# Short rows scattered to first-choice places inside the fused stage; the first pass scatters sums only; both passes run as one stream of 80 pairs

## The chip, the cores and the metric

The kernel runs on one core of one Trainium2 chip. The metric is device time in microseconds (us), the median of three runs. PE is the matrix engine, ACT, DVE and POOL are the scalar, vector and GpSimd engines, and SP is the engine that issues most DMAs (transfers) here. A scatter is an indirect DMA issued by POOL: 128 rows, one per partition, each written to the row of a DRAM tensor that an index in SBUF names.

## The reference

8192 tokens (32 batches of 256) of width 256 go through one layer. Only its second half is touched by the change:

```python
x = x + tanh(g_xattn) * attention(layernorm(x), ctx)      # first stages
y = layernorm(x)                                          # (8192, 256)
scores = softmax(y @ Wg.T); wk, idx = top_k(scores, 2)    # 16 experts, 2 chosen
h = einsum('td,edh->teh', y, W1); h = u * silu(g)         # HID = 128
z = sum over the 2 chosen experts of wk * (h_e @ W2[e])
ys = gated(y @ Ws1) @ Ws2                                 # shared expert
out = x + tanh(g_ffn) * (z + ys)
```

## The kernel before

The program has four stages with a barrier of all engines between them: `prepare` (weights), `attend` (attention, writes x1 to DRAM), `mix` (the fused stage: shared expert, router, placing) and `passes` (routed experts).

**mix** runs 16 steps G of 512 tokens (four tiles of 128). A row in SBUF has ROW = 2 * D + 4 = 516 numbers: the running sum x + shared expert (columns 0 to 255), the normalised y (256 to 511) and a tail of four (token number, first-choice place, and the two weights). The rows lie in NX = 5 buffers `row[G % 5]`. DVE makes the tail: `place(G)` (L1336) computes both places, `weigh(G)` (L1324) the two weights; `add_x1(G)` (L1363) adds the shared expert's output one step later, and its semaphore is `added`. POOL writes the token number (`note`, L1100), makes the low halves of expert G's weights (`low_weights`, L1104, 128x768) and scatters the four tiles of step G-1 to their second-choice places in `rows1` (`scatter`, L1109, the DMA on L1116). SP loads the rows of step G+3 into their buffer once the scatters of step G-2 from that buffer have landed; ACT normalises them (`normalise`, L1243). The order on each engine is written out by hand.

**passes** runs over pairs: a pair q is two tiles of 128 places that each belong to one expert. Pass 1 has pairs 0 to 39 (second choices, from `rows1`), pass 2 pairs 40 to 79 (first choices, from `rows0`). Rows lie in U = 10 buffers `prow`. A step s of the pipeline does, in this order, the transposes of pair s (L1549), the hidden matmuls of pair s-1, the transposes of pair s-2 and the down matmuls of pair s-3 on PE; ACT and DVE split each result in high and low halves; DVE's last operation of a pair (L1666, two instructions, semaphore `final`) adds weight times result to the sum in the row. POOL then scatters: in pass 1 the whole row of 516 to its first-choice place in `rows0`, in pass 2 the sum (256) to `out`. SP loads pair q into buffer q % 10 when pair q-10's scatters have landed. Unused places are covered by blank tiles (`blank_tails`, L1441): 16 for `rows1` at the end of mix, 16 for `rows0` in four groups within pass 1. Between the passes SP waits for every scatter of pass 1, since any tile of `rows0` may hold rows from any of them; PE runs 18 idle matmuls (L349) there. PE's expert addresses are register loads once in ten pairs.

## Time and profile before

| | us |
|---|---|
| median of 3 runs | 992.02 (991.86 to 994.16) |
| the profiled execution | 994.32 |
| its span, first to last instruction | 992.5 |
| mix, from its first POOL instruction to POOL's last scatter | 495.9 to 712.3 |
| pass 1, first transpose to last | 718.6 to 842.2 |
| pass 2, first transpose to last | 862.5 to 970.7 |
| PE busy in the span | 919.1 (93%) |
| POOL busy in the span | 495.0 (50%) |

A profile tells for one execution when each instruction ran on each engine, and what ended an engine's idle time. A busy share over the span mixes stages, so the stages are read apart. "us from issue to landing" is the time from the issue of a DMA to its semaphore. The granted clock (PEclk) is PE's clock as a share of 2.4 GHz. The span leaves out some 2 us around the program that the run's time has.

### The profile page before, as it was taken

To read this page: it belongs to the slowest core of one execution; us is meant where nothing else is said; L and a number is where in the kernel's file an instruction comes from. 1 tells how busy PE (TensorE), PEld (TensorE's weight loads), DVE (VectorE), ACT (ScalarE), POOL (GpSimd) and SP (SyncE) were. 2 spreads that over 40 slices of the span, in tenths; PEclk is the share of its full clock that TensorE was granted. 3 is DMA by queue.
4 is the path that set the end of the run, shared out by engine and by line. 5 is a ranking of instruction groups with operands and counts; after the bars stand their busy time and mean duration, and the time that the engine had idled before them with its cause. 6 is when DMAs were issued, how large, how long until landed. Compare 5 with 4: busy or idle time off the path is not lost. (4 is left out here: it accounts for less than half of the span.)

```text
span 992.5 us, 20889 instructions
## 1 busy us (share of the span) xinstructions
PE 919.1 (93%) x6722; PEld 854.1 (86%) x6722; DVE 806.0 (81%) x1840; ACT 524.2 (53%) x1191; POOL 495.0 (50%) x604
## 2 busy tenths in 40 slices
PE   6699999999999999999779999998797889899994
PEld 6599999999999999998768888887597889699993
DVE  7899999999999999988568989988476568278773
ACT  6577776777777775644254455553043334144441
POOL 4346354453645355343434555554346457457765
PEclk9799999999999999999779999999999889999997
DMA  8213323332233222221153444443799998478880
GB/s 238 73 47 105 91 61 92 92 105 66 86 92 105 71 68 72 70 71 44 38 192 107 171 168 164 169 161 121 273 317 350 336 353 279 148 256 269 264 279 27
DMA packets 108342, 151.15 MB, mean 152 GB/s; under 512 B 21830, under 2 KB 72394, under 8 KB 108240
## 3 DMA queue, kind: packets, MB, share of 16 engines
q1 hardware_dynamic: 92880, 107.60, 35.0%
q0 software_dynamic: 15360, 42.24, 11.2%
q8 instruction: 59, 0.97, 0.4%
q14 instruction: 43, 0.35, 0.1%
HBM read 90.19 MB, written 65.90 MB: 157 GB/s over the span
## 5 line engine op out<-in xcount | busy, mean ns | idle before, releaser
L671 POOL TENSOR_TENSOR prob<-prob,row_sum 128x616 f32<-128x616 f32 x64 | 77.9, 1217 | 141.9 <-DVE row_sum L893 141.9
L1527 POOL DMA_INDIRECT rows_scratch<-prow x80 | 78.7, 984 | 66.2 <-DVE prow L1666 37.2
L1116 POOL DMA_INDIRECT rows_scratch<-row,slot x64 | 67.9, 1061 | 75.4 <-DVE row L1367 60.7
L1527 POOL DMA_INDIRECT out<-prow x80 | 78.7, 984 | 49.7 <-issue 26.8
L1624 ACT ACTIVATE eyT_hi<-ps_ey 128x512 fp32r<-128x512 f32 x80 | 47.9, 599 | 105.2 <-PE ps_ey L1549 105.2
L75 PE MATMUL ps_h<-w_flat,eyT_hi 128*128 x320 | 97.5, 305 | 0.0
L1649 DVE TENSOR_TENSOR eyT_lo<-ps_ey,eyT_hi 128x512 fp32r<-128x512 f32 x80 | 55.3, 692 | 49.0 <-ACT eyT_hi L1624 46.2
L76 PE MATMUL ps_h<-w_flat,eyT_hi 128*128 x320 | 90.6, 283 | 0.0
L77 PE MATMUL ps_h<-w_flat,eyT_lo 128*128 x320 | 90.5, 283 | 0.0
L75 PE MATMUL ps_s<-M_hi,xT_hi 128*128 128x308 f32 x256 | 82.0, 320 | 7.4 <-PEq L387 4.1
L805 ACT ACTIVATE prob<-prob,rstd 128x616 f32<-128x616 f32 x64 | 51.9, 811 | 67.4 <-DVE prob L883 67.4
L261 POOL TENSOR_TENSOR xT_lo<-xT_raw,xT_hi 128x512 fp32r<-128x512 f32 x32 | 41.2, 1287 | 88.2 <-ACT ctxb_hi L227 87.1
L232 DVE TENSOR_TENSOR PT_lo<-ps_pt,PT_hi 77x512 fp32r<-77x512 f32 x128 | 80.2, 666 | 0.0
L75 PE MATMUL ps_o<-PT_hi,V_hi 96*128 96x256 f32 x256 | 76.7, 300 | 3.4 <-DVE PT_lo L232 3.3
L76 PE MATMUL ps_s<-M_lo,xT_hi 128*128 128x308 f32 x256 | 79.0, 308 | 0.0
L77 PE MATMUL ps_s<-M_hi,xT_lo 128*128 128x308 f32 x256 | 78.7, 308 | 0.0
L75 PE MATMUL ps_o<-wo_hi,OT_hi 128*128 128x256 f32 x256 | 75.8, 296 | 1.4 <-DVE OT_lo L232 1.4
L76 PE MATMUL ps_o<-PT_lo,V_hi 96*128 96x256 f32 x256 | 73.4, 287 | 0.0
L77 PE MATMUL ps_o<-PT_hi,V_lo 96*128 96x256 f32 x256 | 73.4, 287 | 0.0
L76 PE MATMUL ps_o<-wo_lo,OT_hi 128*128 128x256 f32 x256 | 73.0, 285 | 0.0
L77 PE MATMUL ps_o<-wo_hi,OT_lo 128*128 128x256 f32 x256 | 72.5, 283 | 0.0
L1666 DVE SCALAR_TENSOR_TENSOR prow<-ps_z,prow 128x256 f32<-128x256 f32 x160 | 69.4, 476 | 1.2 <-PE ps_z L77 1.1
(283 smaller groups left out, 3338.8 us busy)
## 6 DMA issues: line engine op xcount, KB each, us to landing
prow<-rows_scratch SPq DMA_DIRECT2D x160, 258.0 KB, 3.6
rows_scratch<-blank SPq DMA_DIRECT2D x34, 258.0 KB, 3.8
xT_raw<-in_xT SPq DMA_DIRECT2D x32, 256.0 KB, 4.5
x_tok<-in_x SPq DMA_DIRECT2D x32, 256.0 KB, 2.8
x_scratch<-x_tok SPq DMA_DIRECT2D x32, 256.0 KB, 3.1
row<-x_scratch SPq DMA_DIRECT2D x16, 512.0 KB, 3.9
x_ahead<-in_x SPq DMA_DIRECT2D x26, 256.0 KB, 4.4
w_raw<-in_W SPq DMA_DIRECT2D x16, 256.0 KB, 3.5
```

The lines of the kernel that those rows point to most:

```text
L75: nc.tensor.matmul(out, lh, rh, start=start and n == 0, stop=False)
L76: nc.tensor.matmul(out, lh, rl, start=False, stop=False)
L77: last = nc.tensor.matmul(out, ll, rh, start=False, stop=stop and n == len(pairs) - 1)
L232: nc.vector.tensor_tensor(lo, source, f32(hi), ALU.subtract).then_inc(done, 1)
L261: nc.gpsimd.tensor_tensor(a.xT[par][1][:, :, :], a.xT_raw[par][:, :, :], f32(a.xT[par][0][:, :, :]), ALU.subtract).then_inc(a.x_split, 1)
L671: nc.gpsimd.tensor_tensor(pr, pr, row_sum[i][:, :].unsqueeze(2).broadcast_to((P, H, CK)), ALU.mult).then_inc(normed, 1)
L805: nc.scalar.activation(prob[i][:, :], prob[i][:, :], ACT.Exp, scale=c.rstd1[:, bass.ds(2 * b + i, 1)]).then_inc(exp_done, 1)
L1116: pool.indirect_dma_start(c.rows1, bass.IndirectOffsetOnAxis(slot1[:, t:t + 1], 0), row[G % NX][:, i, :], None).then_inc(scattered[G % NX] ...
L1527: pool.indirect_dma_start(dram, bass.IndirectOffsetOnAxis(target, 0), row[u][:, i, 0:columns], None, bounds_check=bound, oob_is_err=False) ...
L1624: nc.scalar.activation(yT[p][0][:, :, :], ps_y[p][:, :, :], ACT.Copy).then_inc(yT_hi, 1)
L1649: V.tensor_tensor(yT[p][1][:, :, :], ps_y[p][:, :, :], f32(yT[p][0][:, :, :]), ALU.subtract).then_inc(yT_lo, 1)
L1666: last = V.scalar_tensor_tensor(row[b][:, i, 0:D], ps_z[p][:, i, :], row[b][:, i, weight:weight + 1], row[b][:, i, 0:D], ALU.mult, ALU.add)
```

## The change

Every token's short row (y and tail, 260 numbers) is scattered to its first-choice place in `rows0` already in mix, by four more scatters per step. Pass 1 then scatters only the sum (256 numbers) to the same place of a new tensor `sums0`. Pass 2 loads both parts apart: short rows need only the buffer, `rows0`'s blanks, and nothing of pass 1; the sums need all of pass 1's scatters, and only DVE's last operation waits for them (`sum_in`). The loops become one stream of 80 pairs, without the idle matmuls between. The blanks in pass 1 cover both tensors, so they are twice as many of half the size. In the last step of mix some DVE and ACT operations change places, and several semaphores are shared that were apart. POOL's loops are written out.

```diff
 (mix, SP and POOL)
-                    wait(sp, scattered[u], 64 * (G // NX))
+                    wait(sp, scattered[u], 128 * (G // NX))
...
+                def scatter_short(G):
+                    pool.wait_ge(noted, G + 1)
+                    pool.wait_ge(weighed, G + 1)
+                    for i in range(4):
+                        pool.indirect_dma_start(
+                            c.rows0, bass.IndirectOffsetOnAxis(tail_of(G)[:, i, 1:2].bitcast(I32), 0),
+                            row[G % NX][:, i, D:], None).then_inc(scattered[G % NX], 16)
+
                 for G in range(STEPS + 1):
                     if G < STEPS:
                         note(G)
                         low_weights(G)
+                    if G == STEPS - 1:
+                        scatter_short(G)
                     if G >= 1:
                         scatter(G - 1)
+                    if G < STEPS - 1:
+                        scatter_short(G)
...
 (blank_tails)
-                queue.dma_start(dram[bass.ds(at, P), :], c.blank[:, :]).then_inc(done, 16)
+                for dram, columns in blanks:
+                    queue.dma_start(dram[bass.ds(at, P), :], c.blank[:, columns]).then_inc(done, 16)
...
 (passes, SP)
-                for u in range(U):
-                    sp.wait_ge(scattered[u], 32 * ROUNDS)
-                sp.wait_ge(c.blanked0, 16 * E)
-                for q in range(PAIRS, 2 * PAIRS):
-                    load(c.rows0, q)
+                sp.wait_ge(c.blanked0, 32 * E)
+                for q in range(PAIRS, PAIRS + U):
+                    load_first_choice(q, False)
+                for q in range(PAIRS, PAIRS + U):
+                    load_sums(q)
+                for q in range(PAIRS + U, LAST):
+                    load_first_choice(q, True)
...
 (passes, POOL)
-                        send(U * j + u, u, c.rows0, ROW, 1, SLOT_ROWS - 1)
+                for q in range(PAIRS):
+                    send(q, c.sums0, 1, SLOT_ROWS - 1)
...
 (passes, PE)
-                for first, idle in ((0, 4), (ROUNDS, 18)):
...
+                busy(nc, c, ps_h[0][:, :, :].rearrange("p i h -> p (i h)"), c.stats2[:, :], 4)
+                for s in range(LAST + 3):
...
 (passes, DVE)
+                        if q >= PAIRS:
+                            v.wait_ge(sum_in[u], 32 * ((q - PAIRS) // U + 1))
```

`load_first_choice(q, sums)` waits for pair q-10's scatters, reads two places in registers (L1509 of the changed kernel, L1503 before) and issues two loads of 128x260 (L1525) and, if `sums`, two of 128x256 (L1528). `load_sums(q)` issues the latter two alone (L1534).

POOL in mix, one step in the middle (before; `row` is a row buffer, `slot` the second-choice places, and L1116 stands four times):

```order
L1102 COPY row<-tokens 128x4 [waits scattered3]
L1107 TENSOR_TENSOR w_flat<-w_raw,w_flat 128x768 [waits caT_lo,expert_w_hi]
L1116 DMA rows_scratch<-row,slot 67712x516 [waits added,noted]
L1116 DMA rows_scratch<-row,slot 67712x516
L1116 DMA rows_scratch<-row,slot 67712x516 [waits added]
L1116 DMA rows_scratch<-row,slot 67712x516
L1102 COPY row<-tokens 128x4 [waits scattered4]
```

The same place of the changed kernel:

```order
L1102 COPY row<-tokens 128x4 [waits scattered3]
L1107 TENSOR_TENSOR w_flat<-w_raw,w_flat 128x768 [waits caT_lo,expert_w_hi]
L1116 DMA rows_scratch<-row,slot 67712x516 [waits added,noted]
L1116 DMA rows_scratch<-row,slot 67712x516
L1116 DMA rows_scratch<-row,slot 67712x516 [waits added]
L1116 DMA rows_scratch<-row,slot 67712x516
L1123 DMA rows_scratch<-row 67712x260 [waits weighed,noted]
L1123 DMA rows_scratch<-row 67712x260 x3
L1102 COPY row<-tokens 128x4 [waits scattered4]
```

Four scatters of 260 columns now stand between a step's scatters and the next step's token numbers and low weights.

SP where pass 2 begins (before; L1503 reads the places of pair 40):

```order
L1503 TENSOR_LOAD rows_at [waits pscattered6,pscattered7,pscattered5,pscattered8,pscattered4,pscattered9,pscattered3,blanked0,pscattered2,pscattered0,pscattered1]
L1506 ISA
L1506 DMA prow<-rows_scratch 128x516
L1506 ISA
L1506 DMA prow<-rows_scratch 128x516
L1503 TENSOR_LOAD rows_at [waits pscattered1]
```

The changed kernel, pair 49's short rows and behind them the sums of pair 40 (pairs 40 to 48 stand above, each with the wait for its own buffer):

```order
L1509 TENSOR_LOAD rows_at [waits pscattered9]
L1525 ISA
L1525 DMA prow<-rows_scratch 128x260
L1525 ISA
L1525 DMA prow<-rows_scratch 128x260
L1509 TENSOR_LOAD rows_at
L1534 ISA
L1534 DMA prow<-sums_scratch 128x256
L1534 ISA
L1534 DMA prow<-sums_scratch 128x256
L1509 TENSOR_LOAD rows_at
```

The wait for all of pass 1 moved from the first load of pass 2 to the place behind the short rows of its first ten pairs.

## Rows read from the trace of the kernel before

**Rows 1.** Busy time of each engine by stretch, us, granted clock, DMA share, GB/s.

```profile
core 0: us, PE busy (x) PEld busy (x) DVE busy (x) ACT busy (x) POOL busy (x), PEclk, DMA share, GB/s
...
700.00:820.00 120.00, 100.78 (x770) 94.66 (x771) 71.65 (x169) 38.77 (x91) 58.57 (x60) 0.94 0.93 326
...
870.00:975.00 105.00, 104.07 (x907) 103.55 (x906) 83.59 (x188) 47.23 (x113) 70.72 (x72) 1.00 0.79 254
```

**Rows 2.** POOL's timeline in mix: start us, us, engine, line, what, idle before, releaser.

```profile
531.30 1.23 POOL L1116 DMA_INDIRECT rows_scratch<-row,slot  x1 [4.02 <-DVE row L1367]
...
549.32 1.86 POOL L1107 TENSOR_TENSOR w_flat<-w_raw,w_flat 128x768 fp32r<-128x768 f32 x1 [0.82 <-ACT w_flat L1237]
555.03 1.00 POOL L1116 DMA_INDIRECT rows_scratch<-row,slot  x1 [3.85 <-DVE row L1367]
...
557.61 0.97 POOL L1116 DMA_INDIRECT rows_scratch<-row,slot  x1 [0.30 <-issue]
558.89 1.39 POOL L1116 DMA_INDIRECT rows_scratch<-row,slot  x1 [0.30 <-issue]
560.27 0.21 POOL L1102 COPY row<-tokens 128x4 int32<-128x4 int32 x1
...
566.99 1.00 POOL L1116 DMA_INDIRECT rows_scratch<-row,slot  x1 [3.85 <-DVE row L1367]
...
711.28 0.97 POOL L1116 DMA_INDIRECT rows_scratch<-row,slot  x1 [0.30 <-issue]
```

**Rows 3.** DVE's timeline under the long scatter of 558.89.

```profile
558.75 1.48 DVE L1354 TENSOR_TENSOR caT_lo<-ca,caT_hi 128x512 fp32r<-128x512 f32 x2
```

**Rows 4.** ACT's normalising of step 15 (timeline), and the landing of its load.

```profile
669.31 2.07 ACT L1250 ACTIVATE row<-row,shift,rstd 128x256 f32<-128x256 f32 x4
...
DMA to landing us min/median/max: 3.7/3.9/7.8
```

**Rows 5.** PE's timeline: transposes of pairs 17, 18, 38 and 39.

```profile
771.87 1.12 PE L1549 MATMUL ps_ey<-ident,prow 128*128 128x128 f32 x4 [5.38 <-DMA prow<-rows_scratch]
776.84 0.60 PE L1549 MATMUL ps_ey<-ident,prow 128*128 128x128 f32 x4
839.45 0.60 PE L1549 MATMUL ps_ey<-ident,prow 128*128 128x128 f32 x4
842.19 0.60 PE L1549 MATMUL ps_ey<-ident,prow 128*128 128x128 f32 x4
```

**Rows 6.** The same: transposes of pairs 0, 40 and 79.

```profile
718.64 0.66 PE L1549 MATMUL ps_ey<-ident,prow 128*128 128x128 f32 x4 [1.13 <-DMA prow<-rows_scratch]
862.53 0.66 PE L1549 MATMUL ps_ey<-ident,prow 128*128 128x128 f32 x4 [0.97 <-DMA prow<-rows_scratch]
970.73 0.60 PE L1549 MATMUL ps_ey<-ident,prow 128*128 128x128 f32 x4
```

**Rows 7.** Timeline, pair 36: DVE's last operation, POOL's second scatter.

```profile
845.29 0.87 DVE L1666 SCALAR_TENSOR_TENSOR prow<-ps_z,prow 128x256 f32<-128x256 f32 x2
...
848.42 0.99 POOL L1527 DMA_INDIRECT rows_scratch<-prow  x1 [0.30 <-issue]
```

**Rows 8.** Chain that ended last, between the passes: start us, us, what.

```profile
856.16 2.10 DMA rows_scratch<-prow
858.47 0.47 SPq L1503
...
860.02 0.47 SPq L1503
...
861.17 3.62 DMA prow<-rows_scratch
```

**Rows 9.** Landings of L1527's scatters: 732 to 800, and 885 to 965.

```profile
DMA to landing us min/median/max: 4.5/6.3/8.2
...
DMA to landing us min/median/max: 2.7/3.7/4.7
```

**Rows 10.** SP's register reads of line L1503, 885 to 965: ns min/median/max.

```profile
L1503 SPq TENSOR_LOAD <-rows_at x27: 468/486/982, 888.5 to 962.1; - x27
```

More of the change, by code:

```diff
@@ L660, in _ @@
                 sp.wait_ge(c.blank_made, 3)
-                blank_rows(c.rows1)
-                blank_rows(c.rows0)
+                for dram, columns in (*c.blanks1, *c.blanks0):
+                    blank_rows(dram, columns)
                 store(B - 1, (B - 1) % 2)
@@ L1477, in passes, with exists @@
             sem("aT_done"), sem("aT_hi"), sem("aT_lo"), sem("z_done"), sem("final"))
-        def rounds(eng, step, first, lag=0):
-            last = first + ROUNDS
-            for j in range(first, last):
-                for u in range(U):
-                    step(U * j + u, u, j)
-            for u in range(lag):
-                step(U * last + u, u, last)
-        def inside(first):
-            return lambda q: not isinstance(q, int) or U * first <= q < U * (first + ROUNDS)
+        def exists(q):
+            return 0 <= q < LAST
         with nc.Block() as block:
@@ L1496, in _, with places, load_second_choice @@
             def _(sp):
-                def load(dram, q):
+                def places(q, registers, name="rows"):
+                    held = [registers.enter_context(sp.register(f"{name}_{q}_{i}")) for i in range(2)]
+                    sp.load(held, c.rows_at[0:1, 2 * q:2 * q + 2])
+                    return [sp.snap(register, donate=True, min_val=0, max_val=ROWS - P) for register in held]
+                def load_second_choice(q):
                     u = q % U
@@ L1500, in load @@
                     with ExitStack() as registers:
-                        held = [registers.enter_context(sp.register(f"rows_{q}_{i}")) for i in range(2)]
-                        first = 2 * q
-                        sp.load(held, c.rows_at[0:1, first:first + 2])
-                        for i in range(2):
-                            at = sp.snap(held[i], donate=True, min_val=0, max_val=ROWS - P)
-                            sp.dma_start(row[u][:, i, :], dram[bass.ds(at, P), :]).then_inc(row_in[u], 16)
+                        for i, at in enumerate(places(q, registers)):
+                            sp.dma_start(row[u][:, i, :], c.rows1[bass.ds(at, P), :]).then_inc(row_in[u], 16)
@@ new lines, in load_first_choice @@
+                def load_first_choice(q, sums):
+                    u = q % U
+                    wait(sp, scattered[u], 32 * (q // U))
+                    with ExitStack() as registers:
+                        at = places(q, registers)
+                        for i in range(2):
+                            sp.dma_start(row[u][:, i, D:], c.rows0[bass.ds(at[i], P), :]).then_inc(row_in[u], 16)
+                        if sums:
+                            for i in range(2):
+                                sp.dma_start(row[u][:, i, 0:D], c.sums0[bass.ds(at[i], P), :]).then_inc(sum_in[u], 16)
@@ L1508, in _, with load_sums @@
+                def load_sums(q):
+                    u = q % U
+                    with ExitStack() as registers:
+                        for i, at in enumerate(places(q, registers, "sums")):
+                            sp.dma_start(row[u][:, i, 0:D], c.sums0[bass.ds(at, P), :]).then_inc(sum_in[u], 16)
                 sp.wait_ge(c.blanked1, 16 * E)
                 for q in range(PAIRS):
-                    load(c.rows1, q)
+                    load_second_choice(q)
                     first = (q - U) * 4 // 6
@@ L1579, in down, with load_weights_at @@
                     last.then_inc(z_done, 1)
-                def load_weights_at(known, place, pairs):
-                    count = 2 * len(pairs)
+                def load_weights_at(first, last):
+                    count = 2 * (last - first)
                     _, at = nc.values_load_multi_w_load_instructions(
-                        c.weights_at[0:1, bass.ds(place, count)], engines=[mybir.EngineType.PE], min_val=0,
+                        c.weights_at[0:1, bass.ds(2 + 2 * first, count)], engines=[mybir.EngineType.PE], min_val=0,
@@ new lines, in load_weights_at @@
+                    return {q: at[2 * (q - first):2 * (q - first) + 2] for q in range(first, last)}
+                busy(nc, c, ps_h[0][:, :, :].rearrange("p i h -> p (i h)"), c.stats2[:, :], 4)
+                for s in range(LAST + 3):
+                    if s % HELD == 0:
+                        known = load_weights_at(s - 1 if s == 0 else s - 3, s + HELD - 1 if s < LAST else s + 1)
+                    if exists(s):
+                        transpose_rows(s)
+                    if exists(s - 1):
+                        hidden(s - 1, known[s - 1])
+                    if exists(s - 2):
+                        transpose_a(s - 2)
+                    if exists(s - 3):
+                        down(s - 3, known[s - 3])
```

249 lines of the change are left out of this document (116 added, 133 removed).

## The prediction

> **What bounds the kernel now.** I read the stages apart, first by busy time in stretches, then PE's timeline at the transposes that open each step, then POOL's and SP's timelines.
>
> In pass 2 PE is the bound: 104.07 us busy in 105 us at full clock [rows 1]. From pair 40 to pair 79 its transposes are 108.20 us apart [rows 6], 39 steps. An undisturbed step is 2.745 us there as at the end of pass 1 (839.45 to 842.19) [rows 5], which is also what the sum takes below. In pass 1 the same 39 steps take 842.19 - 718.64 = 123.55 us [rows 5, 6], 15.3 us more. The reader is to see at pair 17 that PE stood idle (5.38 us) for rows that had not come, and that its transposes then took 1.12 us instead of 0.6 and pair 18 began 4.97 us later, 2.2 us more than a step: after an idle time of 5.4 us the matmuls ran at half the granted clock for most of a step [rows 5]. A second such place follows at pair 29, and a smaller one lies before it at pair 10. The DMA engines are 93% busy at 326 GB/s in that stretch against 79% at 254 GB/s in pass 2 [rows 1]: pass 1 scatters rows twice as wide as pass 2 does, and the landings are 6.3 us against 3.7 [rows 9].
>
> Between the passes, pair 39's transposes at 842.19 and pair 40's at 862.53 lie 20.34 us apart instead of 2.745 [rows 5, 6]. The chain there is: last scatter 856.16, landing 2.10, SP's register read 858.47, load, landing 3.62 after 861.17 [rows 8].
>
> In mix, PE, DVE and ACT share a step of 11.96 us (POOL's first scatters of two steps at 555.03 and 566.99), and POOL has room in it: it waits 3.85 us for DVE before the scatters and 0.82 us for ACT before the low weights [rows 2]. That room is 4.67 us a step.
>
> **The change, part by part.**
>
> *1. Four more scatters per step in mix (costs).* A scatter is 0.97 us and the gap to the next 0.30 us [rows 2]; pass 1's and pass 2's scatters, 516 and 256 columns wide, are also one like the other, so I take the same for 260 columns. Four cost 4 x 1.27 = 5.08 us, more than the room of 4.67. POOL's step, with nothing waited for, is: four wide scatters 555.03 to 560.28 = 5.25, four short ones 5.08, token numbers 0.21, low weights 1.86, and gaps of 0.10 and 0.30 around those [rows 2]: 12.80 us. One thing in it is not fixed. The scatter of 558.89 took 1.39 instead of 0.97 and ended at 560.28, just as DVE's pair of SBUF-only subtractions ended (558.75 + 1.48 = 560.23) [rows 2, 3]; the 5.25 holds one such loss of 0.42 per step. With POOL busy all the time and drifting against DVE, that loss varies between nothing and the whole 1.48. I add 0.15 and take 12.95. So POOL becomes the slowest engine of mix, 1.0 us a step.
> From its first scatter at 531.30 [rows 2] POOL works through 14 steps, 181.3 us, to 712.6; then the short scatters of step 15 and the wide ones of steps 14 and 15, which stand last, 12 x 1.27 + 0.3 = 15.5, end at 728.1. Before, it was 711.28 + 0.97 = 712.25 [rows 2]. The cost is **+15.9 us**; the barrier and pass 1's first load follow POOL's last landing as now. Bounds: 12.80 a step gives +13.8, 13.86 (every step loses the whole 1.48) gives +28.6.
> Who waits behind POOL: the rows of step 15 are loaded when step 10's scatters have landed. Those began at 650.7 (567.0 + 7 x 11.96) and ended at 655.9; with a landing of 2 to 3 us and the load's 3.9 the rows were there at about 662.5, and ACT wanted them at 669.31 [rows 4]. POOL is 1.0 us a step late, about 10 us there, so ACT gets them 3 to 4 us late; the end of the DVE chain moves from 707 to about 711, still before POOL's last scatters. No further cost. The loads of expert weights wait for low weights, with more room than that. The change of order in the last step and the shared semaphores lie under POOL's lateness: nothing.
>
> *2. Pass 1 (gains).* Its scatters halve to the width of pass 2's; its traffic per step is then that of pass 2, and the buffer's round (scatter, landing, SP, load) is that of pass 2, in which PE never waited for rows. Taken as pass 2 goes, PE's 39 steps fall by 15.3 us (its 108.20 holds a start at lower clock like the one that pass 1 will now have, PE having idled for 14 us before it). What could keep some of it: SP's blanks. Four blanks become eight at each of four places, about 0.54 us each (SP's step of 1.55 us less the register read of 0.47, halved [rows 8]), with the read 5 us. The next load then leaves 5.0 - (2.745 - 1.55) = 3.8 us late. In pass 2 a buffer's round is about 22.7 us (transposes to the start of the second scatter 14.5, pair 36: 842.19 - 3 x 2.745 = 833.96 to 848.42 [rows 5, 7]; landing 3.2, SP 1.4, load 3.6) of the 27.45 that ten buffers give, room 4.7. So it just fits; I keep 0.3 us a place, 1.1. **-14.2 us**, bounds -15.3 and -8 (2 us lost at each place).
>
> *3. Between the passes (gains, in part).* Pair 40's transposes follow pair 39's by one step. What is late next is the sum of pair 40. Counted from pair 39's transposes: the second scatter of pair 39 starts at 14.5 [rows 7], lands 3.2 later (between 2.10 in an idle queue and 3.7 [rows 8, 9]), SP reads and issues pair 49's short rows (0.2 + 1.55), then reads and issues the sums of pair 40 (its second issue starts 1.2 later), and they land after about 3.0 (258 KB took 3.62 [rows 8], these are half): 23.6. DVE would want them at 2.745 + 11.33 = 14.1 (pair 36: transposes 833.96, DVE 845.29 [rows 7]). DVE is in order, and behind that operation stands the low half of pair 44, for which PE's hidden matmuls have 1.1 us to spare: PE stands still for 23.6 - 14.1 - 1.1 = 8.4 us, and then runs at half clock as at pair 17, 2.3 us. Pairs 41 to 49 come 1.55 us apart, faster than a step. From pair 39 to pair 79: 40 x 2.745 + 2.0 for four register loads + 8.4 + 2.3 = 122.5 us, against 970.73 - 842.19 = 128.5 now [rows 5, 6]. **-6.0 us**, bounds -10 (landings as in an idle queue, no clock loss) and -2.
>
> *4. SP in pass 2 (may cost).* From pair 50 SP issues four loads a pair instead of two: 0.49 + 4 x 0.54 = 2.65 us [rows 8, 10], plus what the waits cost, against 2.745. It starts that late, having issued twenty sum loads until about 35 us after pair 39's transposes; pair 50's short rows land at about 39 and PE wants them at 41. Register reads reach 0.98 us [rows 10]. **+0.8 us**, bounds 0 and +4.7 (2.9 us a pair, 30 pairs).
>
> *5. The end.* POOL's last scatters follow the last sum as now; the blanks of rows1, the third blank at the end of attend and POOL's unrolled code lie beside other work: nothing.
>
> **Sum.** 15.9 - 14.2 - 6.0 + 0.8 = -3.5 us. From the profiled execution's 994.3: 990.8. The profiled execution stands 2.3 above the median of the three, 992.0, so the median becomes **988.5 us**. Own range of this case: 983 to 994.
>
> **The rivals.**
> A, the port. If a DVE subtraction of two SBUF operands holds POOL off for its whole time wherever it meets it, each step of mix loses 1.48 and not 0.42. For it: the one long scatter of each step ends 0.05 us behind DVE's pair. Against it: the same scatter started within DVE's work and still lost only 0.42, so only its end needs what DVE holds. Price: 14 x (13.86 - 12.95) = 12.7 us: 1001 us, slower than before. It decides as soon as a step takes over 13.2 us. The Trainium skill ("SBUF — State Buffer", "SBUF: two separate sides") says that the port pair which DVE and GpSimd share is an exclusive lock, held for a whole instruction, also against a DVE instruction with two SBUF inputs. By that rule the cost is this rival's whenever the phases fall badly; the trace agrees in that the scatter ended with DVE's work.
> B, SP or the DMA engines bind the passes. SP's blanks delay pass 1 by 2 us a place (+7) or its four loads take 2.9 us a pair (+4). For it: SP's time a pair is within 4% of PE's step. Against: its queue was never late in pass 2. Time 992 to 998, say 995.
> C, the room in the wait for sums is larger and POOL's steps come at 12.8 us: -2 and -4: 982.
> D, the change doesn't take the time off between the passes: DVE's wait stalls PE as long as the barrier did (18 us). It would need the sums 10 us later than counted; 998 us.
>
> **How the numbers follow.** The forecast has 0.52, A 0.13, B 0.15, C 0.14, D 0.06. The range reaches into A and C: 980 to 1000. A measurement tells about 0.3%, 3 us, from no change. Below 989.0 lie C and rather more than half of the forecast's case: faster 0.47. Between 989.0 and 995.0 lie most of its rest and half of B: same 0.30. Slower 0.23.
>
> **What would show it.** POOL's step in mix at 12.8 to 13.1 us with no wait for DVE after the third step, POOL's last scatter at about 728 and pass 1's first transposes at about 734; 39 steps of pass 1 in 108 to 111 us; pair 40's transposes one step behind pair 39's; one PE idle time of 7 to 9 us at pairs 44 to 45, with DVE waiting for a load of sums, and a slow step behind it; pairs 50 to 79 at 2.75 us. It is wrong if POOL's step stays at 12 us (then 972), if short scatters are much cheaper or dearer than 0.97 us, or if PE waits for short rows in pass 2.

## The result and the profile after

The changed kernel took **1010.7 us** (median of 4 runs, 1009.4 to 1011.4) where the kernel before took 991.9 (991.8 to 994.2) on the same chip: a ratio of 1.018, 95% interval 1.0155 to 1.0211. It is 1.8% slower. The forecast was 988.5 us, the range 980 to 1000.

The span of the profiled execution grew by 16.1 us, from 992.5 to 1008.6. Read at the same marks as before, the stages differ by:

| stretch | before, us | after, us | difference | forecast |
|---|---|---|---|---|
| start of mix | 495.94 | 495.09 | -0.85 | 0 |
| mix, to the end of POOL's last scatter | 216.3 | 245.7 | +29.4 | +15.9 |
| from there to pair 0's transposes | 6.4 | 9.0 | +2.6 | 0 |
| pass 1, pairs 0 to 39 | 123.55 | 110.47 | -13.1 | -14.2 |
| pairs 39 to 79 | 128.54 | 126.56 | -2.0 | -5.2 |

So pass 1 did about what was forecast, and mix cost nearly twice the term given for it.

The first view answers rows 1: busy time by stretch, us, then granted clock, DMA share, GB/s. The stages lie later now, so the two stretches don't hold the same work as before.

```profile
core 0: us, PE busy (x) PEld busy (x) DVE busy (x) ACT busy (x) POOL busy (x), PEclk, DMA share, GB/s
700.00:820.00 120.00, 103.47 (x752) 92.70 (x752) 80.61 (x204) 38.50 (x87) 71.20 (x73) 0.96 0.81 270
870.00:975.00 105.00, 93.82 (x789) 91.70 (x788) 73.01 (x165) 41.16 (x99) 64.84 (x67) 0.97 0.77 235
```

In pass 2's stretch PE is now busy 93.82 of 105 us, where it had been 104.07 [rows 1]: it waits there, 6.5 us of it in the one stall that is shown below.

The second view answers rows 2, POOL's timeline in mix: start us, us, engine, line, what, idle before, releaser. L1116 is the wide scatter to the second-choice places, L1123 the new short one.

```profile
569.73 0.20 POOL L1102 COPY row<-tokens 128x4 int32<-128x4 int32 x1
569.88 1.86 POOL L1107 TENSOR_TENSOR w_flat<-w_raw,w_flat 128x768 fp32r<-128x768 f32 x1
573.36 1.01 POOL L1116 DMA_INDIRECT rows_scratch<-row,slot  x1 [1.62 <-DVE row L1380]
...
577.22 1.38 POOL L1116 DMA_INDIRECT rows_scratch<-row,slot  x1 [0.30 <-issue]
578.90 0.97 POOL L1123 DMA_INDIRECT rows_scratch<-row  x1 [0.30 <-DVE caT_lo L1367]
...
582.79 0.97 POOL L1123 DMA_INDIRECT rows_scratch<-row  x1 [0.30 <-issue]
583.75 0.21 POOL L1102 COPY row<-tokens 128x4 int32<-128x4 int32 x1
```

The short scatters cost what was said, 0.97 us and 0.30 between two. But a step is 14.02 us (569.73 to 583.75), not 12.95, and POOL still waits in it, 1.62 us for DVE's sums. An engine that waits in each step doesn't set the step. What DVE does in the same time is in its timeline:

```profile
569.29 0.18 DVE L1346 RECIPROCAL total<-total 128x4 f32<-128x4 f32 x1
569.51 2.27 DVE L1348 TENSOR_SCALAR row<-total,tanh_g 128x4 f32<-128x4 f32 x1
571.81 0.17 DVE L1349 TENSOR_TENSOR row<-over,row 128x4 f32<-128x4 f32 x1
571.89 1.28 DVE L1380 TENSOR_TENSOR row<-ps_co,row 128x512 f32<-128x512 f32 x2
```

L1348 works on four numbers a partition and takes 2.27 us. The groups of instructions by line, 545 to 685 us (count, busy us, mean ns), say the same of all steps; the first row is of the kernel before, the second of the changed one:

```profile
L1333 DVE TENSOR_SCALAR row<-total,tanh_g 128x4 f32<-128x4 f32 x12 | 2.8, 231 | 0.4
```

```profile
L1348 DVE TENSOR_SCALAR row<-total,tanh_g 128x4 f32<-128x4 f32 x10 | 22.5, 2249 | 0.4
```

It began 0.37 us before POOL's low weights (0.22 before the copy of token numbers ahead of them), and it ended at 571.78, 0.04 us after them. The sums (L1380) stand right behind it, and POOL's next scatters wait for the sums.

The last view of this part answers rows 5 and 6: PE's transposes of pairs 0, 39, 40 and 79.

```profile
749.78 0.66 PE L1579 MATMUL ps_ey<-ident,prow 128*128 128x128 f32 x4 [1.16 <-DMA prow<-rows_scratch]
860.25 0.60 PE L1579 MATMUL ps_ey<-ident,prow 128*128 128x128 f32 x4
863.34 0.63 PE L1579 MATMUL ps_ey<-ident,prow 128*128 128x128 f32 x4 [0.19 <-issue]
...
986.81 0.60 PE L1579 MATMUL ps_ey<-ident,prow 128*128 128x128 f32 x4
```

Pair 40 follows pair 39 by 3.09 us in place of 20.34 [rows 5, 6]. The wait that was to take the barrier's place is there: DVE waits for the sum of pair 40, and PE stands behind it and comes back at the lower of its two clock levels. Its matmuls then start 0.21 us apart and read 0.41 us each, against 0.11 to 0.12 apart and 0.28 each at the full level; the granted clock of 884 to 889 us is 0.65. DVE's row first, then PE's:

```profile
882.59 0.88 DVE L1681 SCALAR_TENSOR_TENSOR prow<-ps_z,prow 128x256 f32<-128x256 f32 x2 [7.81 <-DMA prow<-sums_scratch]
```

```profile
884.20 0.58 PE L75 MATMUL ps_h<-w_flat,eyT_hi 128*128 x1 [6.52 <-DVE eyT_lo L1661]
884.57 0.41 PE L76 MATMUL ps_h<-w_flat,eyT_hi 128*128 x1
```

### The profile page after: what moved, and what is told of

Same layout as the page of the kernel before. It is cut to its first block and busy times, and to the rows that moved or that the text cites. A ratio compares the mean times of both kernels' runs of the same rounds, so it can differ in the third digit from the quotient of the medians.

```text
span 1008.6 us, 21133 instructions
## 1 busy us (share of the span) xinstructions
PE 915.1 (91%) x6686; PEld 850.3 (84%) x6686; DVE 833.4 (83%) x1840; ACT 524.7 (52%) x1191; POOL 558.1 (55%) x668
## 5 line engine op out<-in xcount | busy, mean ns | idle before, releaser
L1558 POOL DMA_INDIRECT sums_scratch<-prow x80 | 78.7, 984 | 56.5 <-issue 28.9
L75 PE MATMUL ps_h<-w_flat,eyT_hi 128*128 x320 | 96.3, 301 | 6.5 <-DVE eyT_lo L1661 6.5
L1116 POOL DMA_INDIRECT rows_scratch<-row,slot x64 | 67.9, 1060 | 40.2 <-DVE row L1380 24.9
L76 PE MATMUL ps_h<-w_flat,eyT_hi 128*128 x320 | 89.4, 279 | 0.0
L1123 POOL DMA_INDIRECT rows_scratch<-row x64 | 63.3, 989 | 24.9 <-issue 15.1
```

Source lines behind the costliest of these rows:

```text
L75: nc.tensor.matmul(out, lh, rh, start=start and n == 0, stop=False)
L76: nc.tensor.matmul(out, lh, rl, start=False, stop=False)
L1116: pool.indirect_dma_start(c.rows1, bass.IndirectOffsetOnAxis(slot1[:, t:t + 1], 0), row[G % NX][:, i, :], None).then_inc(scattered[G % NX] ...
L1123: pool.indirect_dma_start(c.rows0, bass.IndirectOffsetOnAxis(tail_of(G)[:, i, 1:2].bitcast(I32), 0), row[G % NX][:, i, D:], None).then_inc ...
L1558: pool.indirect_dma_start(dram, bass.IndirectOffsetOnAxis(target, 0), row[u][:, i, 0:D], None, bounds_check=bound, oob_is_err=False).then_ ...
```

## The experiments

Each is the changed kernel with the edit shown. The runs were made in four groups, each on another chip and beside its own runs of the kernel before (medians 992.3 to 993.8 us), and each ratio is to those; so a difference of 1 to 2 us between medians of two groups says nothing by itself. "Step" is the mean step of mix, from POOL's copies of token numbers between 548 and 685 us.

| kernel | median, us | ratio to before, 95% | step, us |
|---|---|---|---|
| changed | 1010.7 | 1.018 (1.0155 to 1.0211) | 14.02 |
| e1 short scatters first | 991.3 | 0.997 (0.995 to 0.9998) | 12.52 |
| e2 three operands | 1011.6 | 1.017 (1.013 to 1.021) | 14.01 |
| e8 single operand | 1011.7 | 1.020 (1.016 to 1.025) | 14.02 |
| e9 sums ahead of weigh | 1005.9 | 1.013 (1.008 to 1.017) | 13.82 |
| e13 zeros for low weights | 993.5 | 1.001 (0.999 to 1.003) | 12.86 |
| e5 one tensor | 1007.4 | 1.012 (1.008 to 1.017) | 14.01 |
| e7 wide scatters in pass 1 | 1027.0 | 1.033 (1.028 to 1.038) | 14.02 |
| e4 no idle matmuls | 1009.2 | 1.017 (1.012 to 1.021) | 14.02 |
| e10 = e1 + e5 | 986.8 | 0.994 (0.991 to 0.997) | 12.52 |
| e12 = e5, low weights on DVE | 994.1 | 0.999 (0.997 to 1.002) | 12.82 |
| e11 = e10, half of them on DVE | 986.1 | 0.9945 (0.992 to 0.997) | 12.50 |
| e14 = e11 without idle matmuls | 985.7 | 0.993 (0.990 to 0.996) | 12.49 |

### e1: is it a loop of POOL and DVE, or POOL's own work?

```
                         note(G)
                         low_weights(G)
+                    if 1 <= G < STEPS:
+                        scatter_short(G - 1)
                     if G == STEPS - 1:
                         scatter_short(G)
                     if G >= 1:
                         scatter(G - 1)
-                    if G < STEPS - 1:
-                        scatter_short(G)
```

> The changed kernel with one edit: GpSimd sends the four short scatters of group G-1 after the low weights of step G and ahead of the row scatters of G-1 (the changed kernel sends the short scatters of G after the row scatters of G-1). The count of instructions stays. Theory (a loop of two engines: GpSimd's low weights run beside VectorE's tensor_scalar of weigh, which takes 2.25 us instead of 0.23, so the sums come late and GpSimd waits 1.6 us for them in each step): now a short scatter runs beside weigh's chain, the tensor_scalar takes 0.23 us again, GpSimd's step goes from 14.02 to 12.5-13.0 us, its last scatter lands 13 to 20 us earlier, and the kernel takes 991 to 998 us. Rival (GpSimd's own work and its queue need 14 us a step wherever the low weights stand): step 14.0, time 1009 to 1012 us.

Measured: 991.3 us, 19.4 less than the changed kernel, with the same instructions. The timelines of POOL, then of DVE, in e1:

```profile
587.68 0.20 POOL L1102 COPY row<-tokens 128x4 int32<-128x4 int32 x1
587.84 1.86 POOL L1107 TENSOR_TENSOR w_flat<-w_raw,w_flat 128x768 fp32r<-128x768 f32 x1
589.86 1.00 POOL L1123 DMA_INDIRECT rows_scratch<-row  x1 [0.17 <-issue]
...
594.97 0.96 POOL L1116 DMA_INDIRECT rows_scratch<-row,slot  x1 [0.30 <-issue]
```

```profile
588.93 0.19 DVE L1357 TENSOR_TENSOR reached<-ps_r,reached 128x32 f32<-128x32 f32 x1
589.15 0.70 DVE L1359 TENSOR_TENSOR spot<-spot,mask 128x128 f32<-128x128 f32 x1
...
591.72 0.38 DVE L1348 TENSOR_SCALAR row<-total,tanh_g 128x4 f32<-128x4 f32 x1
```

POOL waits for no engine any more: its gaps are the 0.30 of any two scatters. Its own work is 12.50 us a step. L1348 is down to 0.38; what the low weights hold now is L1359 in the end of them (0.70 instead of 0.29), while L1357, which reads from PSUM, passed beside them in 0.19. Pair 0's transposes come at 729.98 instead of 749.78, so the whole gain lies in front of pass 1. The first theory holds, and the rival is out.

### e2, e8 and e13: what does the hold depend on?

e2 rewrites the held instruction with a third operand:

```
-                    link(V.tensor_scalar(tail[:, :, 2], total[:, :], c.tanh_g[:, 1:2], None, ALU.mult))
+                    link(V.scalar_tensor_tensor(tail[:, :, 2], total[:, :], c.tanh_g[:, 1:2], ones[:, 0:4],
+                                                ALU.mult, ALU.mult))
```

> The changed kernel with one instruction rewritten: in weigh, tail[2] = total x tanh_g is a scalar_tensor_tensor with a third operand (ones in bf16) instead of a tensor_scalar. GpSimd's order stays as in the changed kernel. Theory (it is the form of this instruction that lets GpSimd's low weights hold VectorE up: scalar_tensor_tensor and tensor_tensor beside the same GpSimd instruction took 0.28 and 0.17 us): the instruction takes 0.23 to 0.3 us where the tensor_scalar took 2.25, the sums are added 2.0 us earlier in a step, GpSimd's wait of 1.62 us goes, its step is 12.5 to 13.0 us, and the kernel takes 991 to 998 us. Rival (VectorE waits there for something else, a semaphore or SBUF's own queue, whatever the form): the instruction still takes over 2 us and the time stays at 1009 to 1012 us.

Measured: 1011.6 us, and the theory as written fell. The 0.28 and 0.17 us from which it argued are of L1344, which ended 0.87 us before the low weights began (568.73 + 0.28 against 569.88), and of L1349, which began after their end, so neither had lain beside them. Groups by line, as above:

```profile
L1348 DVE SCALAR_TENSOR_TENSOR row<-total,tanh_g,ones 128x4 f32<-128x4 f32 x11 | 24.7, 2241 | 0.4
```

e8 goes the other way, to one operand from SBUF:

```
-                    link(V.tensor_scalar(tail[:, :, 2], total[:, :], c.tanh_g[:, 1:2], None, ALU.mult))
-                    V.tensor_tensor(tail[:, :, 3], over[:, :, E], tail[:, :, 2], ALU.mult).then_inc(weighed, 1)
+                    link(V.tensor_scalar(tail[:, :, 2], total[:, :], 0.5, None, ALU.mult))
+                    V.tensor_scalar(tail[:, :, 3], over[:, :, E], 0.5, None, ALU.mult).then_inc(weighed, 1)
```

> The changed kernel with the last two instructions of weigh reading one operand each: tail[2] = total x 0.5 and tail[3] = over x 0.5, both tensor_scalar with a constant, in place of total x tanh_g (a value per partition from SBUF) and over x tail[2]. It leaves the true gate weights out; counts, order and waits are those of the changed kernel. Theory (a VectorE instruction that reads two operands from SBUF waits until GpSimd's tensor_tensor, which reads two as well, has ended; the run with three operands did not free it, the one-operand RECIPROCAL and TENSOR_REDUCE beside it are never long): neither instruction is held, the sums come 1.6 to 2 us earlier, GpSimd's step is 12.5 to 13.0 us, 991 to 998 us. Rival (what stands in flight when the low weights start is held whatever it reads; the loop finds its place): one of the two takes over 1.5 us again and the step stays at 14.0, 1009 to 1012 us.

Measured: 1011.7 us; the second theory fell too. RECIPROCAL and TENSOR_REDUCE, which it names as never long, end at 569.47 at the latest in the changed kernel's timeline, also before the low weights begin, so whether they would be held isn't shown.

```profile
L1348 DVE TENSOR_SCALAR row<-total 128x4 f32<-128x4 f32 x10 | 22.5, 2249 | 0.3
```

e13 changes POOL's side:

```
-                    g.tensor_tensor(c.w_split[:, e, 1, :], w_raw[e % NW][:, :], f32(c.w_split[:, e, 0, :]),
-                                    ALU.subtract).then_inc(w_lo, 1)
+                    g.memset(c.w_split[:, e, 1, :].bitcast(F32), 0.0).then_inc(w_lo, 1)
```

> The changed kernel with GpSimd writing zeros over each expert's low weights (a memset of 128x768) in place of the subtraction that reads two operands; place, waits and order are the same. It leaves the low halves of the experts' weights out. Theory (what holds VectorE is GpSimd's tensor_tensor with its two reads from SBUF, and nothing else in the order): the memset takes 0.5 to 2 us, no VectorE instruction beside it is longer than in the kernel before, GpSimd's wait for the sums is short or VectorE's own 11.95 us set the step; step 11.95 to 12.5, 982 to 993 us. Rival (any long GpSimd instruction on SBUF holds VectorE, or the place of it does): one VectorE instruction a step still lasts as long as the memset, and the step is over 13 us unless the memset is under 1 us.

Measured: 993.5 us; the theory fell, the rival held. POOL's memset and the DVE instruction beside it, from the two timelines:

```profile
589.38 0.75 POOL L1107 MEMSET w_flat<- 128x768 f32 x1
591.74 0.99 POOL L1115 DMA_INDIRECT rows_scratch<-row,slot  x1 [1.62 <-DVE row L1379]
```

```profile
589.05 1.11 DVE L1347 TENSOR_SCALAR row<-total,tanh_g 128x4 f32<-128x4 f32 x1
```

The memset reads nothing, and it held the same DVE instruction to its own end (590.13 and 590.16), with the same 1.62 us of POOL's waiting. So the hold needs no second operand on DVE's side (e8), and the POOL instruction that it lasts for need not read (e13). Its end is that of POOL's low weights or memset. In all these kernels the held instruction takes its operands from SBUF alone: TENSOR_SCALAR with one or two, SCALAR_TENSOR_TENSOR with three, TENSOR_TENSOR with two. The ones that read PSUM (L1355, 0.28 us, and L1357, 0.19, in e1) were not longer beside the low weights. The Trainium skill ("SBUF — State Buffer", "SBUF: two separate sides") calls the port pair that DVE and GpSimd share an exclusive lock, kept for a whole instruction, for which a DVE instruction competes in a two-port mode or, against a GpSimd instruction that reads SBUF, with two SBUF inputs. The traces agree in that SBUF-only forms were held and PSUM-reading ones not, each to the end of POOL's instruction. For e8 (one tensor operand) and e13 (a POOL instruction that doesn't read) this section of the Trainium skill would need the held TENSOR_SCALAR to have run in a two-port mode; the runs show that it is held, not in which mode it ran. That the shared port is what holds DVE is therefore an explanation by the Trainium skill and is not shown here. What no run explains either is that the record of the held instruction starts 0.37 us ahead of that of the low weights.

### e9: does it matter what stands behind the held instruction?

```
                         place(G)
-                        weigh(G)
                     if G >= 1:
                         add_x1(G - 1)
+                    if G < STEPS - 1:
+                        weigh(G)
```

> The changed kernel with VectorE's adding of the sums (G-1) placed ahead of weigh(G) instead of behind it; GpSimd's order stays. Theory (GpSimd waits for the sums because the held instruction of weigh stands ahead of them on VectorE): the sums pass, GpSimd's wait of 1.62 us goes to under 0.3, what is held behind them costs VectorE alone up to 0.6 us of its slack, GpSimd's step is 12.5 us, 990 to 996 us. Rival 1 (the hold moves ahead of the sums, to place's product of spot and mask, which reads two operands from SBUF): the step is 13.4 to 13.8 us, 1001 to 1008 us. Rival 2 (no hold of VectorE by GpSimd is at work): 14.0 us.

Measured: 1005.9 us, step 13.82: rival 1. The hold moved ahead of the sums (DVE's groups, then POOL's timeline):

```profile
L1359 DVE TENSOR_TENSOR spot<-spot,mask 128x128 f32<-128x128 f32 x10 | 21.6, 2164 | 0.3
```

```profile
595.01 1.83 POOL L1107 TENSOR_TENSOR w_flat<-w_raw,w_flat 128x768 fp32r<-128x768 f32 x1
598.75 1.00 POOL L1116 DMA_INDIRECT rows_scratch<-row,slot  x1 [1.92 <-DVE row L1380]
```

This gives the rule of the loop. DVE's own round of work is the step of the kernel before, 11.96 us [rows 2]; in its timeline its instructions follow one another with one wait of 0.45 us. What a hold or an added instruction puts into that round is added to the step: after 2.25 - 0.23 + 0.05 (L1344, 0.28 instead of 0.23) = 2.07, step 14.03, measured 14.02; e9 2.16 - 0.29 = 1.87, step 13.83, measured 13.82; e13 1.11 - 0.23 + 0.04 = 0.92, step 12.88, measured 12.86. In e1 L1359 is 0.41 longer and L1348 0.16, which gives 12.53, measured 12.52. POOL's own work of 12.50 gives the same there, so e1 doesn't tell which of the two sets its step.

### e12 and e11: taking the low weights from POOL

In e12 DVE makes them, at the end of its step, by the same subtraction (and e5's single tensor is in). The first place is in GpSimd's loop, the second in VectorE's:

```
                         note(G)
-                        low_weights(G)
...
                         choose(G + 1)
                         gaps(G + 1)
+                        low_weights(G)
```

> The changed kernel with one tensor for rows and sums (as in e5) and with all the low weights on VectorE, at the end of each of its steps, instead of on GpSimd; GpSimd's order of scatters stays that of the changed kernel. In e10 GpSimd's step was 12.50 us and its own work set it: eight scatters of 1.27, the copy 0.2, the low weights 1.86. Theory (with no tensor_tensor on GpSimd there is neither a hold nor a GpSimd bound: its work is 10.5 us; VectorE gets about 1.0 us more, from 128x768 at the rate of the 128x512 subtraction's 0.69, in a step of which it is busy 10.8): the step goes back to TensorE's 11.95 us or up to 12.2 and the kernel takes 978 to 983 us. Rival (VectorE's added 1.0 us lies in the chain choose, rank, place that sets the step, or its subtraction waits for ScalarE's high weights): step 12.5 to 13, 986 to 993 us.

Measured: 994.1 us, step 12.82; the theory fell, the rival held. The new instruction costs 0.95 us, of which 0.08 lies over its neighbours:

```profile
L1371 DVE TENSOR_TENSOR w_flat<-w_raw,w_flat 128x768 fp32r<-128x768 f32 x11 | 10.5, 952 | 0.0
```

11.96 + 0.87 = 12.83. DVE's busy share of 0.90 (107.64 of 120 us, 560 to 680, before) had looked like room of 1.2 us a step. There is next to none: a dozen and more small instructions of weigh and choose each wait for the one ahead, with some 0.04 us between, and that counts as idle.

The step is not all that e12's time holds. POOL's last scatter ends at 724.29, but the idle matmuls at the end of mix run until 732.07, and the first work of the next stage starts at 732.4:

```profile
722.07 10.00 PE L349 MATMUL ps_ch<-stats,ident 128*128 128x384 f32 x22
```

From POOL's last scatter to pair 0's transposes it takes 12.3 us, where e1 takes 6.4. e12 without these matmuls was not run.

e11 is e10 with the even experts left on GpSimd and the odd ones on VectorE:

```
                         note(G)
-                        low_weights(G)
+                        if G % 2 == 0:
+                            low_weights(G)
...
+                    if G % 2 == 1:
+                        low_weights(G)
```

> e10 (short scatters first, one tensor) with the low weights of every second expert on VectorE at the end of its step, the others on GpSimd as in e10. Theory (GpSimd's own work binds e10's step; its mean goes to 11.6 us, VectorE's busy time up by 0.5): mean step 11.95 to 12.1 us, 979 to 983 us. Rival (GpSimd's tensor_tensor still holds VectorE for up to 1.9 us every second step, and VectorE has lost its slack): mean step 12.3 to 12.6, 984 to 989 us.

Measured: 986.1 us, mean step 12.50, as much as e10. The rival's time came, but only one half of its mechanism: VectorE has lost its slack, while nothing is held for long. In the step with GpSimd's subtraction that lies beside PSUM work, and L1349, the instruction of weigh that was held before, takes at most 0.37 us. DVE's sum gives the step: for two steps 2 x 11.96 + 0.87 + about 0.2 of lengthened instructions of weigh = 25.0.

### e7: is it the width of the scatter that frees pass 1?

```
-                for q in range(PAIRS):
-                    send(q, c.sums0, 1, SLOT_ROWS - 1)
+                for q in range(PAIRS):
+                    send(q, c.sums0, 1, SLOT_ROWS - 1, ROW)
```

> The changed kernel with pass 1 scattering 516 columns instead of 256 into the tensor of sums (the added 260 columns are not read; the tails blanked there are 516 wide too). Theory (the width of the scattered rows is what makes TensorE wait for loads in pass 1, by landings of 5 to 8 us): pass 1's 39 steps go from 110.5 back to 120-124 us and the kernel takes 1019 to 1025 us. Rival (what speeds up pass 1 is the unrolled program of one stream of 80 pairs, or the order of the loads): the 39 steps stay at 110 to 113 us and the time at 1009 to 1013 us.

Measured: 1027.0 us. Pair 0's transposes are at 749.00, pair 39's here:

```profile
876.80 0.60 PE L1579 MATMUL ps_ey<-ident,prow 128*128 128x128 f32 x4
```

That is 127.8 us for 39 steps against 110.5. The issues of loads, 762 to 830 us (count, KB each, median us to landing), of the changed kernel and of e7:

```profile
prow<-rows_scratch SPq DMA_DIRECT2D x42, 258.0 KB, 3.8
```

```profile
prow<-rows_scratch SPq DMA_DIRECT2D x36, 258.0 KB, 5.0
```

The width is the cause. The unrolled program and the order of the loads alone give nothing: with the old width pass 1 is 4.3 us longer than the 123.55 of before. It writes 32 tails where there were 16, which may be why; single executions also differ (the kernels with narrow scatters took 109.5 to 113.4 us for these 39 steps).

### e5: is SP late in pass 2, or the DMA engines?

```
-                            sp.dma_start(row[u][:, i, D:], c.rows0[bass.ds(at[i], P), :]).then_inc(row_in[u], 16)
-                        if sums:
-                            for i in range(2):
-                                sp.dma_start(row[u][:, i, 0:D], c.sums0[bass.ds(at[i], P), :]).then_inc(sum_in[u], 16)
+                            if sums:
+                                sp.dma_start(row[u][:, i, :], c.rows0[bass.ds(at[i], P), :]).then_inc(row_in[u], 16)
+                            else:
+                                sp.dma_start(row[u][:, i, D:], c.rows0[bass.ds(at[i], P), D:]).then_inc(row_in[u], 16)
```

The scatters go to the same tensor, the short ones at an element offset of 256.

> The changed kernel with short rows and sums in one tensor of 516 columns: the fused stage scatters 260 columns at an element offset of 256, pass 1 scatters 256 columns at offset 0, pairs 40 to 49 load their two parts apart as before, and pairs 50 to 79 load whole rows by two transfers a pair instead of four; the tails are blanked by 16 transfers instead of 32. Theory (SyncE's issue of four transfers a pair, 2.6 us unstretched and 2.95 in the mean, makes pass 2 late): waits of TensorE for loads at pairs 50 to 79 go, pass 2 is 4 to 6.5 us shorter, total 1004 to 1007 us. Rival (the DMA engines' work, which stays the same in bytes, makes the loads late): no change in pass 2, 1009 to 1012 us. The step of GpSimd in the fused stage should stay at 14.0 us by both.

Measured: 1007.4 us. PE's waits for loads in pass 2 (line waited for: us in total, times, longest), changed kernel and e5:

```profile
PE ps_ey L1579 <- DMA prow<-rows_scratch: 5.1, 8, 1.8
```

```profile
PE ps_ey L1579 <- DMA prow<-rows_scratch: 2.8, 1, 2.8
```

The one that is left is pair 50, the first that needs a whole row. From pair 60 (931.99) to pair 79 (984.62) e5 takes 52.63 us and the kernel before 52.67; the changed kernel took 56.60 (930.21 to 986.81). The other kernels with four loads a pair took 53.8 to 56.0 us for this part, and those with two 52.6 to 53.0.

The gain is not whole in e5. From pair 40 to pair 60 it takes 2.8 us longer than the changed kernel (69.71 against 66.87), with the wait of 2.8 us at pair 50, so from pair 40 to pair 79 it is only 1.1 us shorter (122.34 against 123.48) and not the 4 to 6.5 of the theory. On top of e1 (in e10, below) the same edit makes these pairs 5.3 us shorter (118.58 against 123.89).

The bytes are the same, 260 GB/s in this part by both. SP, from pair 60 to pair 79, never waits for a scatter in the changed kernel, and waits 17.8 us for scatters in e5. So SP's queue of issues is what is late in the changed kernel, and with two loads a pair it has room. e5 also halves the packets (12771 to 6765), so why some issues are stretched stays open. In the changed kernel the issues for two pairs read:

```profile
902.58 0.86 SPq L1525 DMA_DIRECT2D prow<-rows_scratch  x2
903.63 1.29 SPq L1528 DMA_DIRECT2D prow<-sums_scratch  x2
905.63 1.18 SPq L1525 DMA_DIRECT2D prow<-rows_scratch  x2
907.01 0.88 SPq L1528 DMA_DIRECT2D prow<-sums_scratch  x2
```

Undisturbed, a pair takes 2.58 us (908.58 to 911.16 further on); stretched issues as these make it 2.93 in the mean of pairs 50 to 79, more than PE's 2.745.

### e4 and e14: the idle matmuls at the end of mix

```
                 last.then_inc(table_rows, 1)
-                busy(nc, c, ps_h[0], c.stats2[:, :], 11)
```

> The changed kernel without the 11 rounds of idle matmuls that TensorE runs on one bank at the end of the fused stage (they keep it busy until the stage ends). Theory (these matmuls, at half clock after GpSimd's late end, run until 745.4 us and hold the barrier between the stages some 1.9 us past the landing of GpSimd's last scatter at 743.5): the gap between GpSimd's last scatter and pass 1's first transposes goes from 9.0 to 6.4-7.2 us, total 1008 to 1010 us, if pass 1's first pairs lose nothing to a low clock. Rival (they buy the clock for pass 1: the granted clock in the first 10 us of pass 1 falls to half and the first ten pairs take 2 to 6 us more): 1011 to 1016 us.

Measured: 1009.2 us. In the changed kernel the granted clock fell to 0.66 in the first 5 us of these matmuls (736 to 741), some of which ran at the lower level, and they ended at 745.38, right ahead of the next stage's first register read at 745.75. Before, at a granted clock of 1.00, they took 7.36 us and ended at 713.85, ahead of the barrier.

```profile
736.33 9.05 PE L349 MATMUL ps_ch<-stats,ident 128*128 128x384 f32 x22
```

Without them the way from POOL's last scatter to pair 0's transposes is 7.7 us instead of 9.0, though the granted clock of 735 to 750 us falls from 0.89 to 0.54. The four other kernels with the changed kernel's step of 14.0 and these matmuls took 8.2 to 9.3, so they cost 0.5 to 1.6 us there. The runs' times can't tell it: the ratios are 1.017 and 1.018. e14 leaves them out of e11:

> e11 (short scatters first, one tensor, every second expert's low weights on VectorE; 986.1 us) without the 11 rounds of idle matmuls at the end of the fused stage, which brought the changed kernel 1.5 us (1009.2). Theory (they hold the barrier only when they run at half clock after a late GpSimd end; in e11 the stage ends with GpSimd's landing or with them, whichever is later): 983.5 to 986 us. Rival (where the stage ends sooner TensorE's clock at the start of pass 1 is worth more than the barrier): 986 to 990 us.

Measured: 985.7 us against e11's 986.1. These runs can't tell the difference from none.

### e10: the two remedies together

The edits of e1 and e5.

> Two edits that helped alone put together: the short scatters of G-1 ahead of the row scatters of G-1 (991.3 us alone, -19.4 against the changed kernel) and one tensor of 516 columns with whole rows loaded from pair 50 on (1007.4 us, -3.3). Theory (the two causes lie in different stages and add up): 988.0 us, 986 to 990, just faster than the kernel before. Rival (the loads' lateness in pass 2 was there only because of something the first edit has taken away, since its own pass 2 has fewer waits for loads): 990 to 992 us, no difference to the first edit alone.

Measured: 986.8 us, ratio 0.994 (0.991 to 0.997): 6 us faster than the kernel before, and 24 faster than the changed one; 19.4 and 3.3 alone would give 22.7. The theory holds, and from pair 60 to pair 79 PE takes 52.9 us where e1 takes 55.2. e10, e11 and e14 beat both kernels and can't be told from one another.

## Why the prediction was wrong

**The step that failed** is the bound of mix, in part 1: "POOL's step, with nothing waited for, is ... 12.80 us", "So POOL becomes the slowest engine of mix". Two things were wrong in it.

First, POOL's idle time was taken as room to be filled. Of the 4.67 us [rows 2] the sum used up 3.85 that was a wait for DVE's sums, as if that wait must shrink when POOL does more. It does so only while DVE's round stays at 11.96, and nothing in the working asked what POOL's work, once it moves, does to DVE. Eight scatters (10.4 us) end, counted from the sums that release them, just when DVE has come round to the end of weigh, the last instructions ahead of the next sums. POOL's copy and low weights fall on them and hold them to their end; the sums come late; the scatters start late by as much, and the next low weights fall on the same place. In the kernel before, with four scatters, the low weights began some 4 us ahead of those instructions and lay beside DVE's work on PSUM. e1 shows this by moving the four scatters alone.

Second, the size. e1 is what the sum meant to price: POOL always at work, no wait. Its step was 12.50 to 12.52 us, the forecast 12.95. So the work was sized well and even too high, and what the forecast left out, the hold on DVE, makes the step 14.02: 1.5 us more than e1's, some 20 us in all.

**Rival A** had the right two engines and the wrong direction: it asked what DVE's SBUF-only work does to POOL, and priced 13.86 us a step. POOL's scatters lose only the 0.42 us as before (577.22, 1.38 us); it was DVE that lost, up to 2 us at one small instruction. Its sign, a step of over 13.2 us, came, but not by its mechanism. It had 0.13. Of the rule that it names (the Trainium skill, "SBUF — State Buffer", "SBUF: two separate sides") it left out a limit: a DVE instruction with two SBUF inputs competes only against a GpSimd instruction that reads SBUF. Whether a scatter is one, no run here tells.

**Pass 1** was right: -13.1 measured, -14.2 forecast, 110.5 us within the 108 to 111 named, by the width of the scatters (e7). In the other kernels with these scatters the 39 steps took 109.5 to 113.4 us, most of them over 111, so landing within the named 3 us was partly luck.

**Between the passes** was right in kind: pair 40 one step behind pair 39, one stall, a slow return of the clock. DVE waited 7.81 us; pair 46 came 11.06 us behind pair 45, so 8.3 more than a step, where 8.4 + 2.3 = 10.7 was forecast.

**SP in pass 2** was mis-sized: +0.8 taken, while pairs 50 to 79 took 85.7 us where the kernel before took 80.5, so +5.2, over the upper bound of 4.7. The other kernels with four loads a pair took 83.8 to 86.5. The time a pair of 2.65 us was right when undisturbed (2.58); the stretched issues of DMAs, which rows 10 gave a hint of for the register reads, made it 2.93, and SP began that part late, so that nothing absorbed it. Whole rows take it back from pair 60 on (e5, e10).

**Between mix and pass 1** nothing was forecast, and 2.6 us came; by e4 some 0.5 to 1.6 of it are the idle matmuls, part of which PE ran at the lower clock. The rest stays open.

In sum, over the forecast of -3.5 us: mix 13.5, less 0.85 that mix began earlier, the way to pass 1 2.6, pass 1 1.1, pairs 39 to 79 3.2, together 19.6, and -3.5 + 19.6 = 16.1, the growth of the span.

Three things stay open. That a shared port is what holds DVE is shown by no run. Whether the copy of token numbers begins the hold ahead of the low weights (L1348 began before both, and would have ended, at its 0.23 us, 0.01 us after the copy began) was not tried apart. And why e9 caught L1359 but the changed kernel let it pass and caught L1348 is explained by phase alone, which was not varied by itself.

## What to carry to other kernels

An engine's idle time in a loop is room only if the wait that makes it can shrink. Ask which engine's own round sets the loop, sum that engine's instructions with the small gaps between chained ones, and see whether the added work, wherever it pushes its neighbours, comes to lie on it.

When GpSimd and VectorE both work on SBUF, place GpSimd's long compute instructions beside VectorE's work on PSUM, and keep them from the instructions just ahead of the one that GpSimd waits for: such a loop finds the bad phase and stays in it. The order of two blocks of GpSimd's work was worth 19 us here, as much as the whole change cost.

## What the runs showed of the hardware

- A GpSimd subtraction of 128x768 (1.86 us) and even a memset (0.75 us) held a VectorE instruction on 128x4 numbers, from 0.23 to 2.25 and to 1.11 us. It was held with one, two or three operands from SBUF, and so was one of 128x128 numbers with two (0.29 to 2.16 us); VectorE instructions that read PSUM were not (0.28 and 0.19 us beside the same subtraction).
- An indirect scatter of 128 rows cost GpSimd 0.97 us and a gap of 0.30 with 260, 256 or 516 columns alike. In time of the queues width did count: with 516 columns in place of 256, the loads beside them landed in 5.0 us instead of 3.8.
- SyncE issued four loads a pair in 2.58 us when nothing came in its way and in 2.93 in the mean, with issues of 0.33 us stretched to as much as 1.84. With two loads a pair pairs 60 to 79 took 52.6 to 53.0 us, with four 53.8 to 56.6.
- The 22 idle matmuls took 7.36 us at a granted clock of 1.00, and 9.05 where it was 0.66 in their first 5 us.
